# Set-up work of a four-layer kernel moved from VectorE to ScalarE: own share, turned diagonals, scaled kernel rows, high halves

## What is computed

```
tc[q,p,i]   = mean_j  tmp[q,p,j,(j+i)%b]      # mean of each wrapped diagonal
w[q,p,r,c]  = tc[q,p,(r-c)%b]                 # every row is the one above, rolled
```

## Time and profile before

| what | value |
|---|---|
| runs | 2843.35, 2843.7, 2851.99 us |
| profiled execution | 2844.92 us, its span 2843.1 us |
| granted TensorE clock, mean | 0.941 |
| TensorE busy | 2312.9 us (81%) |
| VectorE busy | 2243.9 us (79%) |
| ScalarE busy | 1621.7 us (57%) |
| GpSimd busy | 1442.8 us (51%) |
| share of the DMA engines' time | 19.2% |

### The profile page before, as it was taken

How to read it: one execution, slowest core, us unless ns; L and a number is a source line. 1 busy time by engine, 2 the same in 40 slices (tenths; PEclk the granted TensorE clock), 3 DMA queues, 4 the chain that set the end, 5 groups by cost and what they waited for, 6 DMA issues and landing times. The chain is left out here.

```text
span 2843.1 us, 67589 instructions
## 1 busy us (share of the span) xinstructions
PE 2312.9 (81%) x27254; PEld 1321.7 (46%) x27254; DVE 2243.9 (79%) x3739; ACT 1621.7 (57%) x4072; POOL 1442.8 (51%) x1149
## 2 busy tenths in 40 slices
PE   0357738898888988898888978898889988899887
PEld 0233325455554545454554445454554445444454
DVE  7887956888888887888788887888888887886444
ACT  0322037754875567654876467754876567755554
POOL 2414552455735574456635474456635574455344
PEclk9868868999999999999999999999899999999989
DMA  5400400114110421114110411114110421111111
GB/s 150 123 3 15 168 3 17 31 67 142 31 40 25 141 66 32 31 68 142 32 46 24 142 61 32 31 68 142 32 46 24 142 61 32 31 60 46 46 46 39
DMA packets 125431, 176.20 MB, mean 62 GB/s; under 512 B 72496, under 2 KB 114240, under 8 KB 115520
## 3 DMA queue, kind: packets, MB, share of 16 engines
q1 hardware_dynamic: 125120, 171.88, 19.2%
HBM read 98.95 MB, written 72.86 MB: 60 GB/s over the span
## 5 line engine op out<-in xcount | busy, mean ns | idle before, releaser
L2048 PE MATMUL F<-g_raw,cw_hi 128*128 128x512 f16 x2304 | 701.0, 386 | 54.6 <-DVE X L1462 23.0
L1172 ACT ACTIVATE xs<-xs,mx 128x64 f32<-128x64 f32 x1792 | 445.8, 335 | 79.4 <-DVE mx L1813 79.4
L892 POOL TENSOR_TENSOR xs<-xs,rec 128x512 f32<-128x512 f32 x256 | 292.7, 1153 | 344.5 <-DVE rec L1823 343.5
L2048 PE MATMUL F<-g_raw,cw_lo 128*128 128x512 f16 x1152 | 444.0, 385 | 0.0
L2048 PEld LDWEIGHTS F<-g_raw,cw_hi 128*128 128x128 f16 x2304 | 222.0, 99 | 327.0 <-DVE X L1462 30.3
L1179 ACT ACTIVATE prt<-PTR 128x512 f32<-128x512 f32 x256 | 151.4, 591 | 259.2 <-PE PTR L2149 229.7
L877 POOL TENSOR_TENSOR tmp<-X,uw 128x512 f32<-128x512 f32 x128 | 164.4, 1299 | 253.8 <-DVE X L1658 236.2
L907 POOL TENSOR_TENSOR ot_lo<-ot,ot_hi 128x512 f16<-128x512 f32 x128 | 153.7, 1222 | 221.2 <-ACT ot_hi L1193 182.2
L1802 DVE TENSOR_TENSOR xs<-SP,bias 128x1024 f32<-128x1024 f32 (+2 forms) x192 | 160.2, 862 | 117.0 <-issue 67.2
L1391 DVE SCALAR_TENSOR_TENSOR g_raw<-l0c,gn,g_raw 128x512 f16<-128x512 f32 x192 | 183.2, 996 | 55.6 <-ACT g_raw L1031 40.0
L1821 DVE TENSOR_REDUCE sums<-xs 128x16 f32<-128x1024 f32 x128 | 154.9, 1210 | 79.8 <-ACT xs L1167 42.3
(11 more groups left out here) (326 smaller groups left out, 5725.3 us busy)
## 6 DMA issues: line engine op xcount, KB each, us to landing
scratch_x<-X SPq DMA_DIRECT2D x32, 1024.0 KB, 4.8
xs<-scratch_x SPq DMA_DIRECT2D x56, 508.0 KB, 3.4
out_x<-xs SPq DMA_DIRECT2D x56, 508.0 KB, 2.8
X<-in_x SPq DMA_DIRECT2D x25, 1024.0 KB, 6.4
l0c<-scratch_t SPq DMA_DIRECT2D x8, 1876.0 KB, 10.2
l0c<-in_x SPq DMA_DIRECT2D x7, 1024.0 KB, 5.0
l0c<-scratch_t SPq DMA_DIRECT2D x8, 640.0 KB, 12.2
l0c<-scratch_t SPq DMA_DIRECT2D x8, 576.0 KB, 13.5
```

Of the source, the lines that this page charges most:

```text
L892: G.tensor_tensor(keyed(sc[:, u % 4, :]), keyed(sc[:, u % 4, :]), rec[:, u % 4, :].unsqueeze(2).to_broadcast([P, 8, TOK]), ALU.mult).then_ ...
L1172: last = S.activation(keys, keys, ACT.Exp, bias=mx[:, u % 4, i:i + 1])
L2048: last = T.matmul(F[:, n % 2, :], wgt[:, ci, C3 * comp + dx, P * co:P * co + P], win[which], start=(ci == 0 and dx == 0 and j == 0), stop= ...
```

## The change

The own share, the turned diagonals and all high halves go to ScalarE. VectorE's four copies go away: the first sum reads the weight twice. All diagonal sums (`diagonals`) now come ahead of all additions (`circulant`), each block size has its own `tc` and its own turned copy, and the turned copies are written over WB in xs. ScalarE takes six scaled rows out of each bank instead of three, so that VectorE's six combinations give rows that already hold their factors; the high halves are then two copies (four rows and two rows at a time) instead of six, and the low halves two subtractions. The projections' low halves become one instruction each, behind ScalarE's high halves; the w_qkv tiles are no longer scaled in place. In the written order the pieces that are gone are taken out and ScalarE gets five new pieces at norm0b and one at conv12.0; the others keep their places.

The pieces of the set-up on VectorE at each stage, up to the peak, by this order. Before: load (alpha, shares, own share, all of b = 2, b = 4, copy of 8), norm0a (half of the sums of 8), norm0b (rest of them), norm0c (turned 8, additions 8, copy 16), reduce0 to reduce2 (sums 16, turned 16, additions 0 to 3), reduce3, reduce4 (the others), reduce5 (peak). After: load (alpha, shares, sums of 2, 4, 8, half of 16), norm0a (sums 8 to 11), norm0c (sums 12 to 15, additions 2 and 4), reduce0 (additions 8, first half), reduce2 (second half, additions 16 0 to 3), reduce3, reduce4 (the others), reduce5 (peak).

```diff
-    "ACT": {"norm0b": "Y", "reduce13": "Y", ...
+    "ACT": {"norm0b": "YYYYYY", "reduce13": "Y", ...
-        "conv13.1": "HHH", "conv14.1": "H", "conv19.0": "H", "convend": "E"},
-    "DVE": {"load": "UUUCCCCUCCCCCYCUYCCCYYCCCYYYYYYY", "norm0a": "Y", "norm0b": "Y", "norm0c": "YYYY",
-        "reduce0": "YY", "reduce1": "Y", "reduce2": "YYY", "reduce3": "Y", "reduce4": "YY", "reduce5": "Y",
+        "conv13.1": "HHH", "conv14.1": "H", "conv19.0": "H", "convend": "E", "conv12.0": "Y"},
+    "DVE": {"load": "UUUCCCCUCCCCCYCUYCCCYCCCYYYY", "norm0a": "Y", "norm0c": "YYY", "reduce0": "Y", "reduce2": "YY",
+        "reduce3": "Y", "reduce4": "YY", "reduce5": "Y", "reduce6": "U", "reduce7": "U", "reduce9": "U",
...
-KERNEL_ROWS = [(0, 1 / 4), (3, -1 / 6), (4, -1 / 6), (5, 1 / 24), (6, 1 / 24), (2, 1.0)]
...
+        def kernel_parts(n, cw):
+
+            ti, dx = divmod(n, C3)
+            first, second = quarters[2 * (n % 2):2 * (n % 2) + 2]
+            return ((cw[:, ti, dx:dx + 3 * C3 + 1:C3, :], first[:, 0:4, :]),
+                    (cw[:, ti, dx + 4 * C3:dx + 5 * C3 + 1:C3, :], second[:, 0:2, :]))
...
-        tc = tc_both[:, 0:BMAX * BMAX * TAPS]
-        tcr = tc_both[:, BMAX * BMAX * TAPS:2 * BMAX * BMAX * TAPS]
+        level_at = [sum(BMAX * 2 * BMAX // b * TAPS for b in BLOCKS[:n]) for n in range(len(BLOCKS) + 1)]
+        tcs = [tc_both[:, lo:hi] for lo, hi in zip(level_at, level_at[1:])]
+        tcrs = [xs[:, lo:hi] for lo, hi in zip(level_at, level_at[1:])]
+        shares = al[:, 0, 0:len(BLOCKS)]
+        g_quarter, g_sixth, g_24th = (al[:, 1, i:i + 1] for i in range(3))
...
                     yield "alpha"
+                    act.wait_ge(setup_shares, 1)
+                    act.wait_ge(wconv_in, 16 * (P // BMAX))
+                    S.activation(acc, WB, ACT.Copy, scale=al[:, 1, 0:1]).then_inc(setup_own, 1)
+                    yield "own share"
+                    act.wait_ge(setup_tc, 1)
+                    act.wait_ge(setup_own, 1)
+                    for n, b in enumerate(BLOCKS):
+                        src, dst = (ap.rearrange("p (q k c) -> p q k c", k=b, c=TAPS) for ap in (tcs[n], tcrs[n]))
+                        S.activation(dst[:, :, 0, :], src[:, :, 0, :], ACT.Copy, scale=shares[:, n:n + 1])
+                        S.activation(dst[:, :, 1:b, :], src[:, :, b - 1:0:-1, :], ACT.Copy,
+                                     scale=shares[:, n:n + 1]).then_inc(setup_tcr, 1)
+                        yield "turned round"
...
-                        for i in range(C3):
-                            last = S.activation(wu[i], setup_banks(n)[:, i, :], ACT.Copy, scale=gm[:, 4:5])
+                        g0, g1, g2 = (setup_banks(n)[:, i, :] for i in range(C3))
+                        for to, g, scale in ((6, g0, g_sixth), (7, g2, g_sixth), (3, g0, g_24th), (4, g1, g_sixth),
+                                             (0, g0, g_quarter), (5, g2, gm[:, 4:5])):
+                            last = S.activation(wu[to], g, ACT.Copy, scale=scale)
                         last.then_inc(setup_g, 1)
...
-                        for comp, (row, scale) in enumerate(KERNEL_ROWS):
-                            S.activation(cw_hi[:, ti, C3 * comp + dx, :], wu[row], ACT.Copy, scale=scale
-                                         ).then_inc(setup_hi, 1)
+                        for high, rows in kernel_parts(n, cw_hi):
+                            S.activation(high, rows, ACT.Copy).then_inc(setup_hi, 1)
                         yield f"high{n}"
+                    act.wait_ge(setup_q, 1)
+                    for t in range(CT):
+                        S.activation(qkv_hi[:, t, :], qkv_f[t], ACT.Copy, scale=gm[:, 5:6]).then_inc(setup_q_hi, 1)
+                    S.activation(wo_hi[:, :, :], wo, ACT.Copy, scale=wm[:, 2:3]).then_inc(setup_q_hi, 1)
+                    yield "high halves"
...
-                def circulant(n, b):
-
-                    seq.link(V.tensor_copy(diag(tc, b, 0, b), blocks(WB, b, 0, 0, b)))
-                    yield "copy"
+                def diagonals(n, b):
+
                     for j in range(1, b):
...
+                        for lo, count, at_ in ((0, b - j, j), (b - j, j, 0)):
+                            so_far = blocks(WB, b, 0, lo, count) if j == 1 else diag(tcs[n], b, lo, count)
+                            last = V.tensor_tensor(diag(tcs[n], b, lo, count), so_far, blocks(WB, b, j, at_, count), ALU.add)
+                        if j + 1 < b:
+                            seq.link(last)
+                        elif n + 1 == len(BLOCKS):
+                            last.then_inc(setup_tc, 1)
                         if j % 4 == 3:
                             yield "sum"
-                    for i in range(b):
-                        last = V.tensor_scalar(diag(tcr, b, i, 1), diag(tc, b, (-i) % b, 1), al[:, 1, n + 1:n + 2],
-                                               1.0 / b, ALU.mult, ALU.mult)
-                    seq.link(last)
-                    yield "turned round"
+
+                def circulant(n, b):
+
+                    dve.wait_ge(setup_tcr, n + 1)
...
+                    for n, b in enumerate(BLOCKS):
+                        last = V.tensor_scalar(shares[:, n:n + 1], al[:, 1, n + 1:n + 2], 1.0 / b, None, ALU.mult)
+                    last.then_inc(setup_shares, 1)
                     yield "shares"
                     dve.wait_ge(wconv_in, 16 * (P // BMAX))
-                    seq.link(V.tensor_scalar(acc, WB, al[:, 1, 0:1], None, ALU.mult))
-                    yield "own share"
+                    for n, b in enumerate(BLOCKS):
+                        yield from diagonals(n, b)
+                    dve.wait_ge(setup_own, 1)
...
+                    seq.link(V.tensor_scalar(gm[:, 4:5], gm[:, 4:5], FULL, None, ALU.mult))
+                    V.tensor_scalar(g_quarter, gm[:, 4:5], 1 / 4, None, ALU.mult)
+                    V.tensor_scalar(g_sixth, gm[:, 4:5], -1 / 6, None, ALU.mult)
+                    V.tensor_scalar(g_24th, gm[:, 4:5], 1 / 24, None, ALU.mult).then_inc(setup_scaled, 1)
...
+                        V.tensor_tensor(wu[6], wu[6], wu[7], ALU.add)
+                        seq.link(V.scalar_tensor_tensor(wu[7], wu[7], -1.0, wu[3], ALU.mult, ALU.add))
+                        V.tensor_tensor(wu[1], wu[6], wu[4], ALU.add)
+                        V.tensor_tensor(wu[2], wu[6], wu[4], ALU.subtract)
+                        V.scalar_tensor_tensor(wu[3], wu[4], -0.5, wu[7], ALU.mult, ALU.add)
+                        V.scalar_tensor_tensor(wu[4], wu[4], 0.5, wu[7], ALU.mult, ALU.add).then_inc(setup_u, 1)
...
+                        for i, ((low, rows), (high, _)) in enumerate(zip(kernel_parts(n, cw_lo), kernel_parts(n, cw_hi))):
+                            dve.wait_ge(setup_hi, 2 * n + i + 1)
+                            V.tensor_tensor(low, rows, high, ALU.subtract).then_inc(setup_lo, 1)
...
-                    for t in range(CT):
-                        seq.link(V.tensor_scalar(qkv_f[t], qkv_f[t], gm[:, 5:6], None, ALU.mult))
-                        seq.link(V.tensor_copy(qkv_hi[:, t, :], qkv_f[t]))
-                        V.tensor_tensor(qkv_lo[:, t, :], qkv_f[t], qkv_hi[:, t, :], ALU.subtract)
-                        yield "halves"
...
+                    V.tensor_scalar(wm[:, 2:3], wm[:, 2:3], FULL, None, ALU.mult).then_inc(setup_q, 1)
...
+                    yield "scales"
+                    for t in range(CT):
+                        dve.wait_ge(setup_q_hi, t + 1)
+                        V.scalar_tensor_tensor(qkv_lo[:, t, :], qkv_f[t], gm[:, 5:6], qkv_hi[:, t, :], ALU.mult, ALU.subtract)
+                    yield "halves"
+                    dve.wait_ge(setup_q_hi, CT + 1)
+                    V.scalar_tensor_tensor(wo_lo[:, :, :], wo, wm[:, 2:3], wo_hi[:, :, :], ALU.mult, ALU.subtract)
                     dve.wait_ge(setup_tr, CT * C3 + 1)
-                    seq.link(V.tensor_scalar(wo_flat, wo_flat, wm[:, 2:3], None, ALU.mult))
-                    seq.link(V.tensor_copy(wo_hi[:, :, :], wo))
-                    V.tensor_tensor(wo_lo[:, :, :], wo, wo_hi[:, :, :], ALU.subtract)
```

More of the change, by code:

```diff
@@ L62 @@
         "conv23.0": "WWWWRRRRERRRRRRRRRRRRERRRRRRRRRR", "convend": "RR"},
[1 row of a table removed]
[1 row of a table added]
         "hwmean7": "Y", "logits": "YY", "gate3": "Y", "gate11": "Y", "gate16": "Y", "conv3.0": "H", "conv7.0": "H",
[11 rows of a table removed]
[10 rows of a table added]
+        "convend": "VCVJJVVJCVCCVUVVVVVVUEECECCCUUEUECEECUCUUCUEUUEU"},
     "PE": {"reduce13": "Y", "reduce14": "Y", "zpool": "Y", "bandturn": "Y", "hwmean3": "Y", "norm1a": "Y",
@@ L423, in build @@
         setup_perm = sem("setup_perm")
+        setup_shares = sem("setup_shares")
+        setup_own = sem("setup_own")
+        setup_tc = sem("setup_tc")
+        setup_tcr = sem("setup_tcr")
+        setup_q = sem("setup_q")
+        setup_q_hi = sem("setup_q_hi")
         pads_zero = sem("pads_zero")
@@ L1297, in setup @@
```

(25 more changed lines are left out.)

15 lines of the change are left out of this document (5 added, 10 removed), and 17 rows, old and new, of the table FIRST.

## The result

The changed kernel takes 2841.6 us (median of 20 runs, 2837.6 to 2846.5), the kernel before in the same rounds 2846.9 (20 runs, 2843.0 to 2856.0). The ratio is 0.9979, 95% interval 0.9972 to 0.9986: 6.0 us faster, 4.0 to 8.0. That is under 0.3%, the line drawn in the prediction. The forecast, 2835.4 with a range to 2840.5, was 6.2 us too low. 3.2 of these are the start of the sum: it began at 2843.7, a median of three runs, and the kernel before has its median at 2846.9. The other 3.0 are gain that I forecast (8.3) and that did not come (5.3 by medians).

A forecast was written before the change was run, and what follows sets the result against it. The prediction took image 0's serial set-up, through VectorE's circulant work and peak, as the bound. Gains of 7.4 + 0 + 0.9 = 8.3 us from 2843.7 gave 2835.4 us, range 2831 to 2840.5.

The forecast's parts named there:

- What bounds the kernel; where the change acts: Image 0's set-up: weights landed, VectorE's circulant work, peak, all-reduce, row sums, bands, gates, convolution form the chain to shorten.
- Taken before the peak, 12.3 less 4.9: VectorE before the peak: 12.3 us of work removed, 4.9 us of new waits, so the peak starts 7.4 us earlier.
- Behind the peak, 0: After the peak: extra scalars, ScalarE copies, low halves and turn4 net to nothing, bounds +0.5 and -0.5 us.
- Projection weights, 0.9: TensorE's 4.96 us wait at the projection weights shortens by 0.6 to 1.3 us; 0.9 taken.
- The rival of the clock: TensorE's clock stays up after the shorter projection-weight wait: 2.8 us more, gain 11.1, time 2832.6 us; chance 0.25.
- What image 0 gains the whole run keeps: Later images are ordered by semaphores, so image 0's gain, 8.3 us by the sum, reaches the end of the run.
- The base: The time of the kernel before from which the forecast gain was subtracted: a median of 2843.7 us.

The follow-up runs named there:

- double delays: Three extra maximum reductions over all convolution weights on VectorE ahead of the peak reduction: median 2855.9 us on the changed kernel, 2859.8 us on the kernel before.
- early turn: Changed kernel with the first block size's diagonals turned into free gated-input buffer once summed, additions spread over reduce1 and reduce2: median 2836.6 us.
- single delay: Changed kernel with two extra maximum reductions on VectorE, over all and half of the convolution weights, ahead of the peak reduction: median 2851.5 us.
- single delay with the read held back: That delayed kernel with the circulant-weight read and the two projection-weight loads behind it held until VectorE has scaled the peak: median 2850.6 us.
- single delay with the loads held back: That delayed kernel with only the two projection-weight loads held until VectorE has scaled the peak: median 2853.2 us.
- the first alone: Kernel before with only own share and turned diagonals on ScalarE; kernel rows and projection weights as before: median 2841.8 us.
- the whole without the rows: Changed kernel with kernel rows, high halves and low halves put back as before, six instructions each: median 2840.6 us.

## Why the prediction was wrong

- **What bounds the kernel; where the change acts.** Right. The chain landing, circulant work, peak, all-reduce, row sums, convolution holds: what the delays and the early turn put in or took out ahead of the peak (from 15 us later to 4 earlier) reaches the end: by medians 0.9 of it in the two double delays, 1.2 to 1.3 in the early turn and in the single delay with the read held back or not, 1.5 in the single delay with the loads held back, which has a stop of 11.28 us. Of the 7.9 us of the change itself it is 0.7.
- **Taken before the peak, 12.3 less 4.9.** Right: 7.9 from the landing, 7.4 forecast; the waits within 0.2 us. The other half microsecond was not traced to a term.
- **Behind the peak, 0.** Net 0.8 lost in the first pair of profiles, just outside the bounds of 0.5, and 0.6 over two profiles each; two profiles of one kernel differ by 0.7 to 0.9 in this stretch. It is not in the terms that were summed: low0, low2, turn4 and the exponential keep the same distance to within 0.2 us (exponential at 171.65, 6.56 ahead; first low differences at 212.88, 6.43 ahead). In the first pair it is GpSimd's stop of 8.14 us (7.95 in the second profile). The prediction moved the row sums with the all-reduce and took the stop between them as fixed.
- **Projection weights, 0.9.** Somewhat low. First to last convolution matmul took 112.7 to 114.3 us in thirteen profiles with this part, 114.3 to 116.3 in five without, means 113.5 and 115.4. Of these 1.9 us, 1.3 come before TensorE starts again behind the wait (65.4 us from the first convolution matmul, without the part 66.7), and this is the part's: the wait is 3.6 or about 2.0 us with it, 4.96 or 3.3 without. It is the high bound of the sum (1.3). The other 0.6 lie behind the wait and go with the clock. In the changed kernel's profile VectorE's low halves start only 6.49 us ahead (a wait of 2.05 for ScalarE fills the room of the instructions that left), but last 4.96 instead of 5.75. In time the part measured 0.9 (-1.7 to 3.7).
- **The rival of the clock.** The clock stayed up in one profile of the change and not in the other, for the same code, and in nine of the thirteen with the projection part; it stayed up in two of the five without. So it is no property of one kernel. Its price was too high: the rest of image 0's convolution behind the wait takes 49.9 us in the first profile of the kernel before and 48.0 with the clock up, 1.95 us for the forecast 2.8; in the change it is 48.8 against 47.8. The profile of the change in which the clock stayed up took 2842.4 us, not 2832.6.
- **"What image 0 gains the whole run keeps".** This is the step of the mechanism that failed, and 2.7 of the 3.0 us of missing gain are there. Over two profiles each, image 0's last matmul comes 8.1 us earlier (329.4 against 337.6); over 31 executions of the change and the 53 of before beside them the medians differ by 5.4. Where the lead goes is shown for the change: near 1075 and 2350 us, in all four pairs of its two profiles with the two of the kernel before, 1.8 us go each time, because the stretch at 1.2 GHz lasts through the second group of output projections instead of ending before it. What moves the stretches is not shown. The clock is not low for longer: over the seven heads (an image's last convolution matmul to the next one's first) 187.7 and 194.6 us in the change, 194.6 and 187.7 before. The low stretches fall on other work.

  The seven periods add to 2263.9 to 2266.1 us in five profiles of kernels with the old circulant work (one of them delayed by 15 us), and to 2265.9 to 2275.0, mean 2269.8, in thirteen with the new. It is nothing that those images execute, as the change leaves their instructions alone. A shift alone is no explanation that the profiles support: the delayed kernel before has 2265.4. They can't name the part either: the first alone has 2266.2 and the whole without the rows 2273.2, but two kernels that differ only in when two loads start have 2275.0 and 2268.5. The cause stays open. What was not tried: moving only the place of instructions in memory, or profiles in the number that a few microseconds of scatter would need.
- **The base.** This is the larger half of the miss, 3.2 of 6.2 us. Three runs were taken for the median, and two of them (2843.35 and 2843.7) lie in the lowest quarter of the later twenty. With runs from 2843 to 2856 in this set, and from 2839 in another, the median of three can be off by as much as the effect. The sum from the later median would be 2838.6, and the range, moved with it, 2834.2 to 2843.7, would hold the 2841.6 measured.

## What to carry to other kernels

A serial prefix can be summed to half a microsecond from the durations and links of one trace; the run behind it, with its clock of two levels, can't, and changed a gain by 2 or 3 us here. Give such a forecast the width that repeated profiles of the same kernel show behind the changed place. When work goes to an idle engine, look for the buffer that lets it start at the first piece: the 4.0 us that the early turn added to 7.9 had been left in waits, most of it because the result was written over operands still in use. After a change of timing, look at what else starts inside a fixed-looking stop.

## What the runs showed of the hardware

- GpSimd's stop between its all-reduce and its next instruction is no constant: 6.93 to 7.45 us in ten profiles, 7.59 to 8.64 in the six with the peak at 88 to 89.2 us, 11.25 and 11.28 with a large read (2304 KB) running in it, and 7.01 again once that read and the loads behind it were held back (one of the ten).
- The same code reaches the same place with different clocks: of two profiles of the change, one has 0.57 and one 1.00 in the window from 281 to 285 us; of two of the kernel before, the group of output projections near 755 us runs at 0.38 us a matmul in one and at 0.63 in the other. The later images' heads (last convolution matmul to the next image's first) come in a few lengths: the third is 177.3 to 177.5 us in ten profiles and 178.5 to 178.7 in eight.
- ScalarE copies reversed runs of 9 floats, with a scale, at no visible extra cost: 864 reversed columns take 1.04 us, 1152 that are not reversed 1.33, and 4608 in one row 4.14.
